# A gated cross-attention block with a routed FFN: another order of the last tiles, and other ends of the attention

## The chip, the cores and the metric

The program runs on one core of one Trainium2 chip. The metric is the device time of one execution in microseconds. An execution of the kernel before took 836.75 us in the median of three runs (835.48 to 837.84).

## The reference, cut to what matters

```python
# x, ctx: (16, 256, 256); 16 heads of 16; E = 8 experts, TOP_K = 2, H = 1024; all float32
x = x + tanh(g_xattn[0]) * xattn(layernorm(x), ctx, ctx)
x = x + tanh(g_ffn[0])   * moe(layernorm(x))

def xattn(queries, keys, values):
    q, k, v = queries @ Wq + bq, keys @ Wk + bk, values @ Wv + bv      # split in 16 heads
    attn = softmax(q @ k.T / 4)                                        # 256 x 256 for each head
    return (attn @ v) @ Wo + bo

def moe(x):                                                            # 4096 tokens
    logits = x @ Wr + br
    gate = softmax(logits where among the top 2, else -inf)
    y[e] = relu(x @ W1[e] + b1[e]) @ W2[e] + b2[e]
    return sum over e of gate[e] * y[e]
```

## The kernel before, in words

Every product that needs float32 accuracy is made of float16 matmuls of a high part and a low part: a high part is ScalarE's copy to float16, the low part VectorE's difference. "Split" below means this pair of steps.

**Attention stage.** There are 16 batches (NB) of 256 tokens. The function `body(t, par)` of each engine is one turn m = 2t+par; it works on several batches at once. In body m, maxima of the scores of batch m are taken (`scores_max` on TensorE, `reduce` on VectorE, eight steps), the attention of batch m-1 is done (`scores`, ScalarE's `exp`, `attend`, eight steps u), and for batch m-2 the result is turned back, divided, multiplied with Wo, added to x, normed, and its router logits follow (`turn_out`, `attended`, `attended_T`, `output`, `residual`, `norm2`, `norm2_T`, `router`). Maxima use PSUM banks 0-1, scores banks 2-3, `attend` bank 7. Since a step u of `scores` writes the same two banks as the step before, it waits for that step's exp. Body NB (m = 16) has no maxima; it holds the attention of batch 15, and the expert weights that arrive late are split beside it. Batch 15's own remainder follows it, written out by hand together with the first products of tile 0.

GpSimd (POOL) computes norms, adds residuals, and issues indirect DMAs: `send_entry` scatters a token and its gate to the list of its expert, `gather` fetches the normed rows of a tile by its list, `scatter` adds a tile's rows to the output in DRAM. SyncE (SP) issues the other loads and stores in a fixed order. Each engine works through its own queue in order; semaphores tie them.

**Expert stage.** The lists of the experts are cut in 32 big tiles (BIGS) of 256 rows and 7 small tiles (SMALLS) of 128. Before, tiles 0 to 31 are big and 32 to 38 small. `step(j)` of each engine does in TensorE `first(j+1)` (x by W1, eight chunks c, 6 matmuls each) interleaved chunk by chunk with `second(j-1)` (hidden by W2, 8 chunks for each 128 rows), and at chunk 4 `gathered_T(j+2)`, the transposes of a gathered tile. ScalarE applies `relu` to tile j+1 in four parts and makes the high part of tile j+2 (`high_x`). VectorE makes low parts of tile j+2 (`low_x`) and of the hidden of tile j+1 in two halves (`cut_hidden`), and computes the weighted output rows of tile j-1 from PSUM (`result`, once for each 128 rows s). `cut_hidden(j+1)` waits for the second product of tile j-1, whose buffer it overwrites. The hidden buffer halves are freed by the cuts, so `relu` waits for the cuts of the tile before.

The wait that the change touches most is in `second`: before its first chunk it waits for `y_ready`, the end of the result that last used its bank. For big tiles banks 6 and 7 hold s = 0 and 1; small tiles use 6 and 7 in turn (`y_bank`). In a step behind a small tile, `result` stands between the two halves of `cut_hidden`. POOL's step j issues `gather(j+2)`, then `scatter(j-2, 1)`, list entries in the early steps, and `scatter(j-1, 0)`, which waits until the scatter of the tile before has landed. Small tiles have buffer halves and semaphores of their own for gathers (`gather_small`, `xg_half`). At the start of each step an engine reads the expert's number of a tile from the table (`value_load`, lines 1862 and 1864 on TensorE) and addresses the weights by it. The first steps, and those from tile 30 on, are written out; the steps between are a loop.

At the start of the program the keys' product of batch 0 comes first on TensorE, then the transposes of the normed x, the queries' product, batch 1's transposes, and a small product of bv and Wo; VectorE then splits Wo before the first reduction.

Of the kernel before, what the change touches and what calls it, by code (L numbers as in the profile page):

```python
# [23 lines left out]
ALU = mybir.AluOpType  # L24
# [8 lines left out]
P = 128  # L33
# [11 lines left out]
def flamingo(nc, x, ctx_in, g_xattn, g_ffn, Wq, bq, Wk, bk, Wv, bv, Wo, bo, Wr, br, W1, b1, W2, b2, out):  # L45
# [26 lines left out]
    with ctx:  # L72
# [241 lines left out]
        xg_half = [[sem(f"xg_half{i}{h}") for h in range(2)] for i in range(2)]  # L314
# [50 lines left out]

        def lists_at(m, par, first):


            return par == first % 2 and within(m, first, NB + 1)
# [7 lines left out]
        def tiles(eng, step, extra, chain=None, per_step=0):  # L377


            laps = BIGS // 2 - 1  # L380
# [15 lines left out]

        def subs(j):

            return SUB if not isinstance(j, int) or j < BIGS else 1

        def slot_at(j):

            return SUB * j if not isinstance(j, int) or j <= BIGS else SUB * BIGS + j - BIGS

        def subs_to(lap):

            return SUB * lap if not isinstance(lap, int) or lap <= BIGS // 2 else SUB * BIGS // 2 + lap - BIGS // 2

        def half_of(j):

            return (j - BIGS) // 2 % 2

        def y_bank(j, par, s):

            return 6 + (s if subs(j) == SUB else par)
# [27 lines left out]
        def _(sp):  # L443
# [81 lines left out]
            def slot_load(j):  # L525
                wait(sp, slots_full[j % 2], 16 * (j // 2))
                base = sp.value_load(tile_base[0:1, j:j + 1], min_val=0, max_val=LISTED - subs(j) * P)
# [68 lines left out]
            for j in range(EARLY, BIGS):  # L596
                slot_load(j)
            hold(sp, table_ready, 6)
            for j in range(BIGS, NT):
                slot_load(j)  # L600

            hold(sp, y_sent[0], 16 * subs_to((NT + 1) // 2))
            hold(sp, y_sent[1], 16 * subs_to(NT // 2))


        @block.gpsimd
        def _(pool):
# [88 lines left out]
            def gather(j, lap, par):  # L696
                hold(pool, slots_full[par], 16 * (lap + 1))
                wait(pool, xg_full[par], 16 * subs_to(lap))
# [7 lines left out]

            def gather_small(j, par):
                h, turn = half_of(j), (j - BIGS) // 4
                if turn == 0:
                    hold(pool, xg_full[par], 16 * SUB * (BIGS // 2))  # L710
                    hold(pool, gT_done, BIGS - 1 + par)
                else:
                    hold(pool, xg_half[par][h], 16 * turn)
                    hold(pool, gT_done, j - 3)
                hold(pool, slots_full[par], 16 * (j // 2 + 1))
                nc.gpsimd.tensor_copy(gather_idx[par][:, h:h + 1].unsqueeze(2), slots[:, slot_at(j):slot_at(j) + 1, 0:1]).then_inc(idx_ready, 1)
                hold(pool, idx_ready, j + 1)
# [1212 lines left out]
```

## Time and profile before

| | us |
|---|---|
| median of 3 runs (lowest, highest) | 836.75 (835.48, 837.84) |
| the profiled execution | 833.6 |
| its span, first to last instruction | 831.8 |
| TensorE busy in it, over its span | 726.9 (87%) |
| VectorE busy | 609.4 (73%) |
| ScalarE busy | 406.4 (49%) |
| GpSimd busy | 458.8 (55%) |
| mean granted TensorE clock | 0.963 of full |

The profile is of one execution. Busy time of an engine is the union of its instructions; PE is TensorE's matmuls, PEld its weight loads, DVE VectorE, ACT ScalarE, POOL GpSimd. In a timeline each row begins with its start and its duration in us, then the engine, the line of kernel.py, the operation, out<-in and the count of merged instructions; brackets hold the idle time of the engine before it and what ended it. A q behind an engine's name is its sequencer. PEclk is the TensorE clock that was granted, 1.00 being 2.4 GHz and 0.50 1.2 GHz.

### The profile page before, as it was taken

How to read it: one execution, taken by the hardware profiler on the slowest of the kernel's cores; microseconds unless marked ns; L12 is line 12 of the kernel's file. 1: busy time of each engine (PE TensorE's matmuls, PEld its weight loads, DVE VectorE, ACT ScalarE, POOL GpSimd, SP SyncE). 2: the span in 40 equal slices, each digit the busy share in tenths (PEclk: the TensorE clock that was granted, in tenths of full speed). 3: DMA queues.
4: the chain of work that ended last, by engine and by line, in shares of the span. 5: the costliest groups of instructions: out<-in, count | busy, mean ns of one | idle time of the engine just before them, and what ended most of it. 6: DMA issues, size and time to landing. Idle time of an engine off the chain costs nothing.

```text
span 831.8 us, 21356 instructions
## 1 busy us (share of the span) xinstructions
PE 726.9 (87%) x6536; PEld 488.2 (59%) x6537; DVE 609.4 (73%) x1256; ACT 406.4 (49%) x783; POOL 458.8 (55%) x453
## 2 busy tenths in 40 slices
PE   2679999888888888877879999999999999999982
PEld 2335555454555544433657777777777777777761
DVE  5668888889898889996356787667666666676653
ACT  2256777677776767675333333333333333333330
POOL 6224444566565676437447677755655555556522
PEclk9689999999999999997689999999999999999997
DMA  6436656676767665553312232343232222333321
GB/s 188 121 85 207 187 162 183 164 191 173 187 154 172 185 183 162 155 141 114 69 49 46 40 52 46 52 54 52 46 48 46 44 48 46 50 50 49 44 32 20
DMA packets 96790, 85.32 MB, mean 103 GB/s; under 512 B 22257, under 2 KB 86001, under 8 KB 96593
## 3 DMA queue, kind: packets, MB, share of 16 engines
q1 hardware_dynamic: 80752, 65.73, 29.1%
q0 software_dynamic: 15680, 18.69, 14.2%
q8 instruction: 41, 0.67, 0.3%
q14 instruction: 29, 0.23, 0.1%
q10 hardware_dynamic: 288, 0.00, 0.0%
HBM read 53.61 MB, written 30.62 MB: 101 GB/s over the span
## 4 chain that ended last, share of the span: by engine, by line
PE 41%; DVE 19%; issue 16%; DMA 9%; POOL 8%; ACT 4%; POOLq 1%; DVEq 0%; ACTq 0%; SPq 0%
PE banks L1765 10%; DMA out_dram<-yb,dest_idx 7%; DVE negmax L1119 7%; PE banks L1661 5%; POOL xg L704 4%; PE banks L1747 4%; PE banks L1749 4%; PE banks L1748 4%; PE banks L1577 3%; ACT probs L931 2%; PE banks L1649 2%; PE banks L1563 2%; POOL out_dram L778 2%; DVE stats L1043 2%; PE banks L1702 2%
## 5 line engine op out<-in xcount | busy, mean ns | idle before, releaser
L994 ACT ACTIVATE hid<-banks,b_col 128x256 f32<-128x256 f32 (+1 forms) x312 | 124.2, 452 | 219.3 <-PE banks L1749 112.9
L1765 PE MATMUL banks<-wall,hh 128*128 x568 | 204.8, 380 | 1.4 <-DVE hl L1458 1.0
L778 POOL DMA_INDIRECT out_dram<-yb,dest_idx x71 | 124.8, 1757 | 126.8 <-DMA out_dram<-yb,dest_idx 58.5
L1119 DVE TENSOR_REDUCE negmax<-banks 128x4 f32<-128x1024 f32 x128 | 155.7, 1217 | 20.7 <-PE banks L1628 20.0
L1747 PE MATMUL banks<-xh,wall 128*128 128x256 f16 (+1 forms) x624 | 163.2, 266 | 5.2 <-ACT hid L994 4.3
L931 ACT ACTIVATE probs<-banks 128x1024 f32<-128x1024 f32 x128 | 131.1, 1024 | 71.8 <-PE banks L1649 70.8
L1749 PE MATMUL banks<-xh,wall 128*128 128x256 f16 (+1 forms) x624 | 163.2, 266 | 0.0
L1748 PE MATMUL banks<-xl,wall 128*128 128x256 f16 (+1 forms) x624 | 163.2, 266 | 0.0
L1765 PE MATMUL banks<-wall,hl 128*128 x568 | 144.3, 273 | 0.0
L1661 PE MATMUL banks<-probs,vaug 128*32 128x256 f32 x1024 | 84.4, 402 | 26.1 <-ACT probs L931 15.3
L689 POOL DMA_INDIRECT token_lists<-entry,place_i x64 | 69.2, 1082 | 66.4 <-ACT probs L931 41.9
L704 POOL DMA_INDIRECT xg<-xn_rows,gather_idx x64 | 77.8, 1215 | 30.4 <-issue 18.1
L1458 DVE TENSOR_TENSOR hl<-hid,hh 128x1024 f16<-128x1024 f32 (+1 forms) x78 | 88.2, 1130 | 2.7
L1507 DVE SCALAR_TENSOR_TENSOR yb<-banks,b_b 128x256 f32<-128x256 f32 x71 | 30.1, 424 | 74.1 <-PE banks L1765 73.8
L1748 PEld LDWEIGHTS banks<-xl,wall 128*128 x624 | 61.6, 99 | 33.0 <-issue 0.3
L1765 PEld LDWEIGHTS banks<-wall,hh 128*128 128x128 f16 x568 | 55.6, 98 | 30.9 <-issue 2.5
L1747 PEld LDWEIGHTS banks<-xh,wall 128*128 x624 | 61.8, 99 | 14.7 <-issue 7.2
L1628 PE MATMUL banks<-ks,qs 48*128 48x256 f16 x512 | 51.0, 278 | 22.1 <-DVE negmax L1119 21.8
L628 POOL TENSOR_TENSOR var_eps<-mean_var,eps_col 128x2 f32<-128x2 f32 x32 | 7.1, 223 | 106.9 <-DVE mean_var L1048 106.9
L1749 PEld LDWEIGHTS banks<-xh,wall 128*128 x624 | 61.7, 99 | 6.6
L1765 PEld LDWEIGHTS banks<-wall,hl 128*128 128x128 f16 x568 | 55.7, 98 | 13.0 <-issue 0.3
L1456 DVE CAST hh<-hid 128x1024 f16<-128x1024 f32 (+1 forms) x78 | 50.8, 651 | 9.2 <-PE banks L1765 7.8
(203 smaller groups left out, 1177.6 us busy)
## 6 DMA issues: line engine op xcount, KB each, us to landing
raw<-in_L_ffn_W SPq DMA_DIRECT2D x16, 512.0 KB, 5.7
wst<-in_L_ffn_W SPq DMA_DIRECT2D x16, 512.0 KB, 6.4
k_parts<-kparts SPq DMA_DIRECT2D x48, 128.0 KB, 5.5
q_parts<-qparts SPq DMA_DIRECT2D x48, 128.0 KB
ks<-k_parts SPq DMA_DIRECT2D x64, 96.0 KB, 2.3
qs<-q_parts SPq DMA_DIRECT2D x64, 96.0 KB, 2.2
xin<-in_x SPq DMA_DIRECT2D x16, 256.0 KB, 2.9
cin<-in_ctx SPq DMA_DIRECT2D x16, 256.0 KB, 3.3
```

Source lines behind the costliest of these rows:

```text
L689: nc.gpsimd.indirect_dma_start(list_d, bass.IndirectOffsetOnAxis(place_i[:, kk, i:i + 1], 0), entry[:, kk, i, :], None).then_inc(list_sent ...
L704: nc.gpsimd.indirect_dma_start(xg[par][:, s, :], None, rows, bass.IndirectOffsetOnAxis(gather_idx[par][:, s:s + 1], 0)).then_inc(xg_full[p ...
L778: nc.gpsimd.indirect_dma_start(out_rows, bass.IndirectOffsetOnAxis(dest_idx[par][:, s:s + 1], 0), yb[par][:, s, :], None, compute_op=ALU.a ...
L931: nc.scalar.activation(probs[v % 2][:].rearrange("p h t -> p (h t)"), banks[:, 2:4, :].rearrange("p b t -> p (b t)"), ACT.Exp, scale=float ...
L994: ins = nc.scalar.activation(hid[half][:, c % (HC // 2), 0:subs(j) * P], banks[:, b, c % 2 * TS:c % 2 * TS + subs(j) * P], ACT.Relu, bias= ...
L1119: nc.vector.tensor_reduce(negmax[:, c, 8 * (g // 2):8 * (g // 2) + 8].rearrange("p (m g p2) -> p m g p2", m=2, g=2)[:, :, g % 2, :], banks ...
L1458: nc.vector.tensor_tensor(hl[par][:, cs, 0:rows], hid[half][:, :, 0:rows], hh[par][:, cs, 0:rows], ALU.subtract).then_inc(hl_ready, 1)
L1661: ins = nc.tensor.matmul(banks[32 * j:32 * j + 32, 7, 0:L], vaug[par][:, c, 8 * (j // 2) + 2 * g + j % 2, :], probs[v_ % 2][:, j, :], star ...
L1747: nc.tensor.matmul(dst, hi, xh[par][:, m, 0:rows], start=(m == 0), stop=False)
L1748: nc.tensor.matmul(dst, hi, xl[par][:, m, 0:rows], start=False, stop=False)
L1749: ins = nc.tensor.matmul(dst, lo, xh[par][:, m, 0:rows], start=False, stop=(m == M - 1))
L1765: ins = nc.tensor.matmul(dst, h_[:, c, s * P:(s + 1) * P], w_, start=(c == 0 and k == 0), stop=(c == HC - 1 and k == 1))
```

## The change

The expert stage:

- Tiles 0 to 24 are big; from tile 25 on small and big tiles alternate (25, 27, ... 37 small, 26, 28, ... 38 big). `MIXED` is 25. The table keeps its order; `entry_of(j)` finds the entry of tile j. The loop ends at tile 22, later steps are written out.
- Results of s = 0 are always in bank 6, those of s = 1 in bank 7; `y_bank` goes. `second` waits for the result of the tile before in the same bank.
- `gather(j+3)` is issued in POOL's step j, behind `scatter(j-2, 1)` and the list entries, ahead of `scatter(j-1, 0)`. `gather_small` and its semaphores go.
- In a step behind a small tile, VectorE's `result` stands behind both halves of `cut_hidden`.
- `gathered_T` stands at chunk 2 instead of 4 where tile j+1 is small.

The end of the attention:

- In body NB the scores alternate between banks 2-3 and 0-1, and `scores(u+1)` is issued before `attend(u)`; `gathered_T(0)` moves from step 6 to 3, ScalarE's `high_x(0)` from 7 to 5. ScalarE's copy for the router (`norm2_T`) and `spread` leave the body. The late weight splits 6 and 7 are one or two steps later.
- POOL's `residual(14)` is ahead of two entry sends.
- Behind the body, the first products of tile 0 are spread between `turn_out`, `norm2_T`, `attended_T`, `router` and `output`; `low_x(1)` comes ahead of the statistics of batch 15; `high_x(1)` ahead of the last `relu`.

The start:

- Norm transposes of batch 0 are ahead of its keys' product; the bv by Wo product moves ahead of batch 1's transposes and to bank 7; statistics of batch 1 are earlier.
- The maxima of batch 0 alternate between banks 0-1 and 2-3, each waiting for the reduction two steps back.
- Splitting Wo moves into body 0, behind its sixth reduction; `output(0)` waits for it instead of `v(0)`.

```diff
+        def score_bank(m, v):
+            return 2 if not isinstance(m, int) or m < NB or v % 2 == 0 else 0
+        def out_bank(n, c):
+            return 5 + c if not isinstance(n, int) or n < NB - 1 or c == 0 else 3
+        def max_bank(n, w):
+            return 2 if isinstance(n, int) and n == 0 and w % 2 else 0
...
-            laps = BIGS // 2 - 1
+            laps = (MIXED - 2) // 2
...
+        MIXED = NT - 2 * SMALLS
+        def smalls_to(j):
+            return max(0, j - MIXED + 1) // 2 if isinstance(j, int) else 0
         def subs(j):
-            return SUB if not isinstance(j, int) or j < BIGS else 1
+            return 1 if isinstance(j, int) and j >= MIXED and (j - MIXED) % 2 == 0 else SUB
...
+        def entry_of(j):
+            return j - smalls_to(j) if subs(j) == SUB else BIGS + smalls_to(j)
...
+                last = isinstance(m, int) and m == NB
+                if last:
+                    residual(m - 2)
                 if sending:
                     paced(here[0], 0)
                     paced(here[1], 2)
-                if post:
+                if post and not last:
                     residual(m - 2)
...
-                if not fixed or 2 <= j < BIGS - 2:
-                    gather(j + 2, t + 1, i)
-                elif j >= BIGS - 2:
...
+                if there(j, 3) and not (fixed and j < 1):
+                    gather(j + 3, t + 1 + i, 1 - i)
                 if there(j, -1):
                     scatter(j - 1, 1 - i, 0, t + (i - 1) // 2)
...
             relu(0, e, 0)
+            relu(0, e, 1)
+            norm2_T(NB - 2)
             attended_T(NB - 1)
-            for b in range(1, 4):
-                relu(0, e, b)
+            relu(0, e, 2)
             high_x(1, 1)
+            relu(0, e, 3)
+            spread(NB // 2 - 2)
...
             dve.wait_ge(biases_ready, 1)
+            norm1_stats(1, 0, 1)
+            norm_low(0)
             k_low(0, 5)
-            norm_low(0)
-            norm1_stats(1, 0, 1)
             q_low(0, 6)
             context_low(1, 1)
+            norm_low(1)
             split_whole(wv, xres, wv_full, wv_high, wv_split)
-            norm_low(1)
...
+                    if w == 5 and isinstance(m, int) and m == 0:
+                        output_weights()
...
             attended(n, 1)
-            router(n - 1, 0, 7)
             attended_low(n)
             cut_hidden(0, 0, 0)
+            router(n - 1, 0, 7)
             residual(n)
+            low_x(1, 1)
             norm2_stats(n)
             cut_hidden(0, 0, 1)
-            low_x(1, 1)
...
                 for half in range(2):
                     if there(j, 1):
                         cut_hidden(j + 1, 1 - i, half)
-                    if half == 0 and after_small and there(j, -1):
-                        result(j - 1, (j - 1) // 2, 1 - i, 0, e)
+                if there(j, -1) and after_small:
+                    result(j - 1, t + (i - 1) // 2, 1 - i, 0, e)
...
-                wait(pe, mx_red, 8 * n + w)
+                wait(pe, mx_red, 8 * n + w if not isinstance(n, int) or n else w - 1)
...
+                if v_ == 0 and isinstance(n, int) and n == 0:
+                    pe.wait_ge(mx_red, 8)
+                if not isinstance(n, int) or n < NB - 1 or v_ == 0:
+                    wait(pe, exp_done, 8 * n + v_)
+                elif v_ == 1:
+                    pe.wait_ge(mx_red, 8 * NB)
+                else:
+                    pe.wait_ge(exp_done, 8 * n + v_ - 1)
...
-                    if subs(j) == SUB:
-                        wait(pe, y_ready, slot_at(j - 1) + s + 1)
-                    else:
-                        pe.wait_ge(y_ready, slot_at(j - 2) + 1 if j - 2 >= BIGS else slot_at(BIGS - 1) + 1 + par)
+                    wait(pe, y_ready, slot_at(j - 1) + (s + 1 if s < subs(j - 1 if isinstance(j, int) else j) else 0))
...
+            norm_T(0)
             for m in range(M):
                 k(0, 0, m, 5)
-            norm_T(0)
...
+                last = isinstance(m, int) and m == NB
                 for u in range(8):
-                    if attention:
+                    if last and u == 0:
+                        scores(m - 1, 1 - par, 0)
+                    if last and u < 7:
+                        scores(m - 1, 1 - par, u + 1)
+                    elif attention and not last:
                         scores(m - 1, 1 - par, u)
...
-            turn_out(n, 0)
-            turn_out(n, 1)
-            router(n - 1, None, 7)
             pe.wait_ge(table_ready, 2)
             pe.wait_ge(late_lo, len(LATE))
             e = pe.value_load(tile_expert[0:1, 0:1], min_val=0, max_val=E - 1)
             first(0, 0, e, 0)
             first(0, 0, e, 1)
-            attended_T(n)
+            turn_out(n, 0)
+            turn_out(n, 1)
             first(0, 0, e, 2)
             first(0, 0, e, 3)
+            norm2_T(n - 1)
+            attended_T(n)
+            first(0, 0, e, 4)
+            first(0, 0, e, 5)
+            router(n - 1, None, 7)
             output(n, 0)
             output(n, 1)
-            for c in range(4, HC):
-                first(0, 0, e, c)
             gathered_T(1, 0, 1)
+            first(0, 0, e, 6)
+            first(0, 0, e, 7)
...
-                    if there(j, 2) and c == HC // 2:
+                    if there(j, 2) and c == (HC // 2 if not isinstance(j, int) or subs(j + 1) == SUB else 2):
```

## Rows read from the trace of the kernel before

**Rows 1.** the page: engines' busy time (share), and the last chain by engine

```profile
PE 726.9 (87%) x6536; PEld 488.2 (59%) x6537; DVE 609.4 (73%) x1256; ACT 406.4 (49%) x783; POOL 458.8 (55%) x453
...
PE 41%; DVE 19%; issue 16%; DMA 9%; POOL 8%; ACT 4%; POOLq 1%; DVEq 0%; ACTq 0%; SPq 0%
```

**Rows 2.** stages: busy us (count) of PE, PEld, DVE, ACT, POOL; PEclk, DMA share, GB/s

```profile
377.40:402.60 25.20, 18.39 (x139) 8.87 (x138) 11.98 (x31) 14.72 (x22) 19.04 (x23) 0.70 0.31 83
402.60:429.90 27.30, 21.71 (x154) 18.30 (x155) 13.17 (x26) 8.83 (x21) 9.40 (x14) 0.81 0.29 78
429.90:761.70 331.80, 329.67 (x2539) 248.99 (x2540) 227.04 (x472) 116.94 (x271) 204.70 (x166) 1.00 0.30 47
...
778.00:811.50 33.50, 29.24 (x327) 21.92 (x324) 19.61 (x48) 13.53 (x45) 12.07 (x10) 1.00 0.26 34
```

**Rows 3.** timeline, TensorE, big tiles: start us, us, what, [idle before <-releaser]

```profile
691.26 0.60 PE L1733 MATMUL banks<-ident,xg 128*128 128x128 f32 x4
...
702.13 0.60 PE L1733 MATMUL banks<-ident,xg 128*128 128x128 f32 x4
```

**Rows 4.** timeline, TensorE, two small steps

```profile
781.10 0.38 PE L1733 MATMUL banks<-ident,xg 128*128 128x128 f32 x2
...
788.06 0.38 PE L1733 MATMUL banks<-ident,xg 128*128 128x128 f32 x2
```

**Rows 5.** a table load (line L1864) and the weight loader, in one small step's boundary

```profile
L1864 PEldq TENSOR_LOAD <-tile_expert x1: 296/296/296, 783.6 to 783.6; - x1
...
784.40 0.10 PEld L1747 LDWEIGHTS banks<-xh,wall 128*128 x1 [1.33 <-issue]
```

**Rows 6.** timeline, VectorE and ScalarE, around the last big tile but one

```profile
751.09 0.42 DVE L1507 SCALAR_TENSOR_TENSOR yb<-banks,b_b 128x256 f32<-128x256 f32 x1 [2.59 <-PE banks L1765]
...
752.41 0.69 DVE L1456 CAST hh<-hid 128x1024 f16<-128x1024 f32 x1
...
754.27 0.69 DVE L1456 CAST hh<-hid 128x1024 f16<-128x1024 f32 x1
...
754.49 0.84 ACT L994 ACTIVATE hid<-banks,b_col 128x256 f32<-128x256 f32 x2 [3.11 <-DVE hl L1458]
```

**Rows 7.** timeline, VectorE, one small tile

```profile
783.57 0.43 DVE L1456 CAST hh<-hid 128x512 f16<-128x512 f32 x1 [1.21 <-PE banks L1765]
...
784.64 0.21 DVE L1505 TENSOR_SCALAR dest_f<-slots,filler 128x1 f32<-128x1 f32 x1
...
786.19 0.42 DVE L1456 CAST hh<-hid 128x512 f16<-128x512 f32 x1
```

**Rows 8.** what the gathered transposes (L1733) waited for in the tile stage: us, times

```profile
  DMA xg<-xn_rows,gather_idx: 5.7, 9
```

**Rows 9.** stretches of 4 us between attention and tiles, columns as in rows 2

```profile
414.00:418.00 4.00, 1.47 (x14) 1.15 (x11) 3.23 (x8) 2.02 (x5) 2.27 (x3) 1.00 0.82 295
418.00:422.00 4.00, 3.35 (x21) 2.48 (x22) 0.59 (x1) 0.36 (x1) 3.51 (x4) 0.63 0.18 63
...
426.00:430.00 4.00, 2.00 (x17) 1.66 (x15) 3.90 (x7) 1.42 (x4) 0.00 (x0) 0.91 0.00 0
430.00:434.00 4.00, 4.00 (x22) 2.57 (x22) 3.18 (x20) 0.43 (x2) 1.89 (x2) 0.66 0.02 4
```

**Rows 10.** timeline, last batch: an exp on ScalarE, and TensorE before the first ranks

```profile
389.77 1.02 ACT L931 ACTIVATE probs<-banks 128x1024 f32<-128x1024 f32 x1 [1.06 <-PE banks L1649]
...
418.65 0.19 PE L1710 MATMUL banks<-picked,tri 128*128 128x32 bf16 x1 [3.18 <-DVE xl L1447]
```

**Rows 11.** timeline, the end: VectorE after step 37, the last scatter on POOL

```profile
811.50 0.43 DVE L1456 CAST hh<-hid 128x512 f16<-128x512 f32 x1 [3.02 <-PE banks L1765]
...
823.51 1.54 POOL L778 DMA_INDIRECT out_dram<-yb,dest_idx  x1 [3.05 <-DMA out_dram<-yb,dest_idx]
```

**Rows 12.** timeline, TensorE, maxima of batch 0 and of batch 1

```profile
26.21 0.39 PE L1628 MATMUL banks<-ks,qs 48*128 48x256 f16 x4 [1.53 <-DVE negmax L1119]
...
41.93 0.61 PE L1628 MATMUL banks<-ks,qs 48*128 48x256 f16 x4 [0.99 <-DVE negmax L1119]
```

More of the change, by code:

```diff
@@ L595, in _ @@
             hold(sp, table_ready, 4)
-            for j in range(EARLY, BIGS):
+            for j in range(EARLY, MIXED):
                 slot_load(j)
             hold(sp, table_ready, 6)
-            for j in range(BIGS, NT):
+            for j in range(MIXED, NT):
                 slot_load(j)
-            hold(sp, y_sent[0], 16 * subs_to((NT + 1) // 2))
-            hold(sp, y_sent[1], 16 * subs_to(NT // 2))
+            hold(sp, y_sent[0], 16 * subs_to((NT + 1) // 2, 0))
+            hold(sp, y_sent[1], 16 * subs_to(NT // 2, 1))
         @block.gpsimd
@@ L968, in body @@
                             values(m, par)
+                        if isinstance(m, int) and m == NB:
+                            high_x(0, 0)
                     elif v == 6:
@@ L973, in body @@
                     elif v == 7:
-                        if isinstance(m, int) and m == NB:
-                            high_x(0, 0)
-                        if post:
+                        if post and not (isinstance(m, int) and m == NB):
                             norm2_T(m - 2)
@@ L981, in body @@
                     copy_out(3)
-                if lists_at(m, par, LEAD):
+                if lists_at(m, par, LEAD) and within(m, 0, NB - 1):
                     spread(t - 2)
@@ L1088, in attended @@
                 dve.wait_ge(tok_done, 2 * n + c + 1)
-                rows = bank(5 + c).rearrange("p (h w) -> p h w", w=32)
+                rows = bank(out_bank(n, c)).rearrange("p (h w) -> p h w", w=32)
                 link(nc.vector.reciprocal(recip[c][:].unsqueeze(2), rows[:, :, DH:DH + 1]))
@@ L1500, in result @@
                 if s == 0:
-                    wait(dve, y_sent[par], 16 * subs_to(lap))
+                    wait(dve, y_sent[par], 16 * subs_to(lap, par))
                     dve.wait_ge(slots_full[par], 16 * (lap + 1))
@@ L1682, in output @@
                     pe.wait_ge(cT_split, n + 1)
+                    if isinstance(n, int) and n == 0:
+                        pe.wait_ge(wo_split, 1)
                 i = 0
@@ L1816, in body @@
                             output(m - 2, 0)
+                        if last:
+                            gathered_T(0, 0, 0)
                     elif u == 4:
@@ L1829, in body @@
                         attend(m - 1, 1 - par, u)
-                    if u == 6 and isinstance(m, int) and m == NB:
-                        gathered_T(0, 0, 0)
-                    if u == 7 and post:
+                    if u == 7 and post and not last:
                         norm2_T(m - 2)
```

108 lines of the change are left out of this document (40 added, 68 removed).

## The prediction

> **What bounds the kernel now.** I read the page first: TensorE is busy 87% of the span, and the chain that ended last runs 41% over it [rows 1]. Then the stages [rows 2]: in the expert stage up to 761.7 it is busy 329.67 of 331.80 us, so there only TensorE work counts. The time that can move lies at its two ends. In the last seven tiles (all small) it is busy 29.24 of 33.50 us; in the last attention batch 18.39 of 25.20 us at a granted clock of 0.70; between attention and the steady tiles 21.71 of 27.30 at 0.81.
>
> Two big tiles in a step (first product of tile j+1, second of tile j-1) take 10.87 us between one set of transposes and the next [rows 3]. Without some 0.44 us of transposes (0.60 with the pipeline's latency) that is 1.30 us for each of eight chunks, half of it (0.65) from either product. In a small step both halve: 0.66 x 8 + 0.22 = 5.5 us. The trace shows 6.96 [rows 4], 1.46 more. The weight loader stands 1.33 us at the boundary, with nothing the profile names as releaser, while the sequencer runs two table loads, of which one is shown [rows 5]. In a big step the queued matmuls cover them. That pause stands four times behind small steps, 5.8 us in all.
>
> **The new tile order.** Small tiles are now 25, 27, ... 37. Since a step joins j+1 and j-1, steps do not mix sizes: even steps 26 to 36 are small with small, odd ones big with big. TensorE work is unchanged. What changes is a wait: all results of s=0 now use bank 6, so `second` of a big tile behind a small one waits at its first chunk for the small tile's result, and the change puts that result last on VectorE, behind both cuts. Before, small tiles took banks 6 and 7 in turn and this wait fell a step later.
>
> I follow one pair from t=0, the end of a big step. VectorE first finishes that step's second result, 1.3 us (751.09 to 752.41), and cuts the big tile, 1.86 a half [rows 6]: 5.1. ScalarE's activations of the small tile wait for those halves, as at 754.49 [rows 6], so the next split of x ends near 5.9. TensorE's small step ends at 5.7 and only that releases the small cuts. These take 1.07 each (783.57 to 784.64), the result 1.55 (784.64 to 786.19) [rows 7]: 5.9 + 2.1 + 1.6 + wake-ups 0.3 = 9.9. TensorE wants to start that product at 5.7 + 0.65 = 6.35. It stands 3.6 us, which includes the table-load pause. Queued behind the waiting matmul are all other first products of the step, so nothing fills the hole. Six pairs: +21.6. Gone are the four old pauses: -5.8. Bounds for a pair: 1.5 (only the old pause) and 4.2 (slower ScalarE links).
>
> **The end.** The last tile is now big: 2.6 us of its second product move behind step 37, so that step ends 2.6 earlier. Before, step 37 ended at about 811.4 (VectorE starts at 811.50), the last scatter was issued at 823.51, and the span ended 8.3 later [rows 11]: 20.4. Now, from the end of step 37: result 1.4, two big cuts 3.7, small result 1.6, wake 0.2 = 6.9; second product 5.3 = 12.2; last half result 1.4 and wake 0.2 = 13.8; last scatter, then 8.3: 22.1. So +1.7 - 2.6 = -0.9. A scatter waits for the landing of the tile before (1.54 + 3.05 us [rows 11]); that stays inside this chain. Bounds -2.6 and +1.5.
>
> **Gathers three ahead.** `gather(j+3)` stands behind `scatter(j-2, 1)` instead of `gather(j+2)` before it, and is a step earlier. The copy of indices, two gathers of about 1.1 us each and the entry sends share the POOL queue, busy 204.70 of 331.80 us in the tile stage [rows 2]; slot loads on SP come one tile earlier and were far ahead. The loader waited for gathers nine times, 5.7 us in all [rows 8]; the matmuls already queued cover about half. I take -2.9; bounds 0 and -5.7.
>
> **The clock.** After a stretch of 4 us with 1.47 us busy, TensorE's granted clock fell from 2.4 to 1.2 GHz (0.63 in the next stretch), and again after 2.00 of 4 busy (0.66) [rows 9]. A new hole is 3.6 us idle with one chunk inside it, of the same kind. The mean of 0.63 over 4 us is about 3 us at half clock; work done in it takes 1.5 to 1.7 longer. Behind it the big step is TensorE-bound, so the loss stays: 6 x 1.7 = +10.2. Bounds 0 and +16.
>
> The Trainium skill ("TensorE: Matmul & The Clock Gate", section "HAM oscillation") describes a kernel that goes back to the slow clock in every tile because of a wait between bursts. That rule speaks against this change; without it the sum would be 10.2 lower, with it as above. The trace agrees as far as the two stretches show.
>
> **The last attention batch.** In batch 15's attention the maxima are done, so scores alternate between banks 2-3 and 0-1 and are issued a turn ahead. Before, each exp waited for its scores: 1.06 us idle before an exp of 1.02 [rows 10], about 2.1 a turn, 2.4 with a copy-out. Now exps follow at ScalarE's pace, 1.0 to 1.4 a turn. Five late turns save about 4; the gathered transposes move from turn 6 to 3 and no longer stand before the last scores (1.5); the last copy-out is not behind the router's activation copy (0.8); 0.7 more in the early turns: -7. TensorE still has router and transposes in turns 0 to 2, and the product with Wo in turn 3 waits for VectorE's late weight split, so it is not more. POOL's residual moves ahead of two entry sends; those were not waited for.
>
> Behind it, first products of tile 0 are put between `turn_out`, `attended_T`, `router` and `output`, each of which waited for ScalarE or VectorE, and the split of tile 1 comes before the statistics and the last cut. At 418.65 TensorE had waited 3.18 us for that split [rows 10]. This wait goes almost wholly; some 2 us of half clock go with the denser work: -5. Late next is the norm of batch 15: VectorE's statistics, then POOL's norm, then router 15 before step 1, so of step 0 only 1 us goes. Together -13. Bounds -5 (clock low all through) and -16.
>
> **The start.** Maxima of batch 0 alternate between two bank pairs, which removes waits as that of 1.53 us before the second [rows 12]; VectorE becomes the bound, with eight reductions, its splits, and now the five operations of the output weights between the sixth and the seventh instead of ahead of the first. Batch 0's scores come earlier by about 1.4, and the 0.99 us wait of batch 1's first maxima [rows 12] goes: -2.4. Norm before keys shortens the query chain, but the first matmuls at half clock come later too; I count nothing for it. Bounds +1 and -5.
>
> **The sum**, against the profiled execution (span 831.8, 833.6 with what lies around it): 21.6 - 5.8 - 0.9 - 2.9 + 10.2 - 13 - 2.4 = +6.8, so 840.4. The median shown is 3.15 above that execution; on it, 836.75 + 6.8 = 843.5.
>
> **Rivals.**
> A. The clock stays up through the holes. For it: the old pauses of 1.3 us left it at 1.00 [rows 2]. Against: rows 9. It decides at whether the hole counts as one. 843.5 - 10.2 = 833.3, just faster than before.
> B. The result of a small tile doesn't hold TensorE, because VectorE gets to it in time. For it: VectorE is busy only 20 of 33.5 us in the small stage [rows 2]. Against: the order of its queue. It decides if the result is out by 6.4 us of the pair. Then holes and clock loss go: 843.5 - 21.6 - 10.2 = 811.7; with old pauses in six small steps 818.
> C. The two ends give little, since each is held by a chain that moves only as a whole (row loads on SP at the start, POOL's norm at the end): -5 in place of -15.4. 854.
> D. The edits at the attention's ends change nothing at all, and clock loss is at its upper bound: 865. I give it almost nothing.
>
> **Chances.** Forecast 0.50, own range 838 to 849. A 0.20 (829 to 837). B 0.12 (808 to 822). C and D 0.18 (849 to 862). The range 829 to 855 leaves out B, and half of C: 0.2. From no change 0.3% (2.5 us, about what can be told here) gives the limits 834.2 and 839.3. Faster: B, a bit over half of A, a little of the forecast: 0.26. Same: 0.14. Slower: 0.60.
>
> **What would show it.** In the changed kernel's trace: six waits of `second` on VectorE's result behind small tiles, each 2 to 3 us after a table pause of about 1, with pair periods near 20 us or 21.7 with the clock; granted clock below 1.00 in stretches from step 27 on; no waits on gathers; exps of the last batch following at 1.0 to 1.4 us; the first ranks of the tile stage 12 to 15 us earlier relative to the start. It is wrong if the pair period stays below 18.5 us, or if the ends give under 8 us or over 20.

## The result and the profile after

The changed kernel takes 851.95 us (median of 4 runs, 849.88 to 853.39), the kernel before 837.07 on the same chip (4 runs, 835.48 to 837.84): ratio 1.0178, 95% interval 1.0150 to 1.0206, 14.9 us slower. I had forecast +6.8. The direction was right, the size was not. The profiled execution takes 852.82 us, its span is 850.7 and its mean granted clock 0.954.

The page of the changed kernel: TensorE's row, the last chain by engine (to be read against [rows 1]), and the group of second-product matmuls.

```profile
PE 735.8 (86%) x6536; PEld 488.5 (57%) x6537; DVE 604.0 (71%) x1256; ACT 404.6 (48%) x783; POOL 461.4 (54%) x453
...
PE 57%; DVE 26%; issue 9%; ACT 3%; DMA 1%; POOL 1%; DVEq 1%; SPq 0%; POOLq 0%; ACTq 0%
...
L1769 PE MATMUL banks<-wall,hh 128*128 x568 | 211.8, 392 | 22.7 <-DVE yb L1515 22.7
```

The same 6536 matmuls are busy 8.9 us longer, and the second product now waits 22.7 us for VectorE's `yb`, the result, which the group of before didn't. Both belong to the tile order. Next, the timeline of TensorE: five of the six waits that I had counted behind small tiles, then the seventh, behind the last small tile and ahead of the last tile.

```profile
703.92 0.57 PE L1769 MATMUL banks<-wall,hh 128*128 x1 [3.20 <-DVE yb L1515]
...
725.63 0.60 PE L1769 MATMUL banks<-wall,hh 128*128 x1 [3.01 <-DVE yb L1515]
...
748.43 0.61 PE L1769 MATMUL banks<-wall,hh 128*128 x1 [3.09 <-DVE yb L1515]
...
792.84 0.60 PE L1769 MATMUL banks<-wall,hh 128*128 x1 [3.10 <-DVE yb L1515]
...
814.48 0.61 PE L1769 MATMUL banks<-wall,hh 128*128 x1 [3.00 <-DVE yb L1515]
...
834.05 0.61 PE L1769 MATMUL banks<-wall,hh 128*128 x1 [4.30 <-DVE yb L1515]
```

From 703.92 to 792.84 lie four pairs, 22.2 us each (forecast 20, or 21.7 with the clock). The product itself lasts 0.6, where it lasts 0.39 at full clock (e3 and e9 below). VectorE ahead of the wait at 748.43:

```profile
743.60 0.68 DVE L1451 SCALAR_TENSOR_TENSOR xl<-banks,xh 128x512 f16<-128x512 f32 x1
744.39 0.43 DVE L1460 CAST hh<-hid 128x512 f16<-128x512 f32 x1
744.85 0.69 DVE L1462 TENSOR_TENSOR hl<-hid,hh 128x512 f16<-128x512 f32 x1
745.46 0.42 DVE L1460 CAST hh<-hid 128x512 f16<-128x512 f32 x1
745.91 0.69 DVE L1462 TENSOR_TENSOR hl<-hid,hh 128x512 f16<-128x512 f32 x1
746.52 0.21 DVE L1509 TENSOR_SCALAR dest_f<-slots,filler 128x1 f32<-128x1 f32 x1
...
747.81 0.35 DVE L1515 TENSOR_SCALAR yb<-yb,slots 128x256 f32<-128x256 f32 x1
```

Two cuts, then the result, with no idle time between: the chain of my forecast. The stages after, with the columns of [rows 2]: up to tile 25's transposes, up to the first wait, the six pairs, the end.

```profile
421.20:670.70 249.50, 248.27 (x1917) 188.16 (x1918) 172.34 (x379) 87.34 (x203) 160.24 (x135) 0.99 0.33 48
670.70:703.90 33.20, 29.81 (x273) 22.61 (x271) 22.59 (x46) 11.54 (x32) 17.95 (x15) 1.00 0.31 49
703.90:834.00 130.10, 109.26 (x840) 77.19 (x840) 63.46 (x132) 35.87 (x98) 49.99 (x41) 0.88 0.22 33
834.00:850.70 16.70, 6.86 (x32) 3.55 (x32) 2.76 (x8) 0.00 (x0) 4.66 (x3) 0.70 0.21 25
```

A mean of 0.88 over 130.1 us, at levels of 1.0 and 0.5, is 31 us at half clock, 5.2 a pair. It comes in pieces of two lengths in turn, as behind the first and the second wait:

```profile
703.00:708.00 5.00, 4.08 (x19) 2.48 (x20) 0.53 (x2) 0.84 (x2) 3.58 (x4) 0.66 0.31 45
724.00:732.00 8.00, 6.37 (x28) 3.80 (x29) 1.30 (x4) 0.84 (x2) 3.76 (x4) 0.57 0.27 51
```

That is 3.4 us at half clock behind one wait and 6.9 behind the next. The kernel before, from its tile 25's transposes to its end, for the same 1144 or 1145 matmuls:

```profile
680.30:831.80 151.50, 132.00 (x1144) 98.36 (x1144) 91.11 (x187) 49.20 (x130) 73.65 (x60) 0.97 0.28 42
```

After, the same stretch (the last three stages above) takes 180.00 us, with TensorE busy 145.93. So of 28.5 us more, in 13.9 TensorE is busy longer with the same matmuls, and 14.6 are idle time.

From the profile after alone the ends seem to give little: tile 1's first product starts at 421.20, 8.7 us earlier than before (429.90 in [rows 2]; I had forecast 15.4), and there is a new wait in the last attention batch. First that wait, then exps of batch 15 on ScalarE after, then the first and the last of them before:

```profile
390.03 1.25 PE L1698 MATMUL banks<-wo,cT 128*128 128x256 f16 x5 [3.53 <-DVE cT L1069]
```

```profile
380.40 1.02 ACT L929 ACTIVATE probs<-banks 128x1024 f32<-128x1024 f32 x1
...
387.98 1.02 ACT L929 ACTIVATE probs<-banks 128x1024 f32<-128x1024 f32 x1
...
393.75 1.02 ACT L929 ACTIVATE probs<-banks 128x1024 f32<-128x1024 f32 x1
...
396.59 1.03 ACT L929 ACTIVATE probs<-banks 128x1024 f32<-128x1024 f32 x1
```

```profile
379.19 1.03 ACT L931 ACTIVATE probs<-banks 128x1024 f32<-128x1024 f32 x1
...
398.46 1.02 ACT L931 ACTIVATE probs<-banks 128x1024 f32<-128x1024 f32 x1 [2.86 <-PE banks L1649]
```

Five exps follow the one before at 1.2 to 1.9 us, one after 2.71 and one only after 5.77: 16.2 us from first to last, where it was 19.3. One trace is a weak measure of the ends, though: the profiled execution of before was 3.5 us faster than its median.

### The profile page after: what moved, and what is told of

The parts are those of the page before. It is cut to its first block, busy times and chain, and to the rows that moved or that the text cites. A ratio compares the mean times of both kernels' runs of the same rounds, so it can differ in the third digit from the quotient of the medians.

```text
span 850.7 us, 21021 instructions
## 1 busy us (share of the span) xinstructions
PE 735.8 (86%) x6536; PEld 488.5 (57%) x6537; DVE 604.0 (71%) x1256; ACT 404.6 (48%) x783; POOL 461.4 (54%) x453
## 4 chain that ended last, share of the span: by engine, by line
PE 57%; DVE 26%; issue 9%; ACT 3%; DMA 1%; POOL 1%; DVEq 1%; SPq 0%; POOLq 0%; ACTq 0%
PE banks L1769 20%; PE banks L1757 7%; PE banks L1755 6%; DVE negmax L1120 6%; PE banks L1756 6%; PE banks L1671 4%; PE banks L1581 3%; DVE hl L1462 2%; PE banks L1659 2%; DVE hh L1460 2%; ACT probs L929 2%; PE banks L1567 2%; PE banks L1714 2%; DVE stats L1044 2%; PE banks L1631 2%
## 5 line engine op out<-in xcount | busy, mean ns | idle before, releaser
L1769 PE MATMUL banks<-wall,hh 128*128 x568 | 211.8, 392 | 22.7 <-DVE yb L1515 22.7
L1120 DVE TENSOR_REDUCE negmax<-banks 128x4 f32<-128x1024 f32 x128 | 155.5, 1217 | 22.6 <-PE banks L1631 22.2
L1769 PE MATMUL banks<-wall,hl 128*128 x568 | 148.8, 281 | 0.0
L1671 PE MATMUL banks<-probs,vaug 128*32 128x256 f32 x1024 | 84.0, 400 | 23.0 <-ACT probs L929 14.6
L718 POOL DMA_INDIRECT xg<-xn_rows,gather_idx x71 | 82.2, 1158 | 26.7 <-issue 15.5
L1659 PE MATMUL banks<-qs,ks 49*128 49x256 f16 x512 | 51.1, 280 | 1.9 <-DVE negmax L1120 1.9
```

The lines of the kernel that those rows point to most:

```text
L718: nc.gpsimd.indirect_dma_start(xg[par][:, s, :], None, rows, bass.IndirectOffsetOnAxis(gather_idx[par][:, s:s + 1], 0)).then_inc(xg_full[p ...
L1120: nc.vector.tensor_reduce(negmax[:, c, 8 * (g // 2):8 * (g // 2) + 8].rearrange("p (m g p2) -> p m g p2", m=2, g=2)[:, :, g % 2, :], banks ...
L1671: ins = nc.tensor.matmul(banks[32 * j:32 * j + 32, 7, 0:L], vaug[par][:, c, 8 * (j // 2) + 2 * g + j % 2, :], probs[v_ % 2][:, j, :], star ...
L1769: ins = nc.tensor.matmul(dst, h_[:, c, s * P:(s + 1) * P], w_, start=(c == 0 and k == 0), stop=(c == HC - 1 and k == 1))
```

## The experiments

Unless said otherwise, a number is the ratio to the kernel before with its 95% interval (5 rounds). 0.001 is 0.84 us. Each kernel ran beside the kernel before, on several chips in all; where I give a difference of two kernels, it is that of their ratios.

**Which part costs what.** Two kernels split the change in two: `e1_ends` takes the start and the last attention batch from the changed kernel and leaves tile order and gathers as before; `e2_tiles` does the reverse.

> The kernel before with the changed start and the changed last attention batch with what follows it, and with its own tile order and gathers (two ahead, seven small tiles last). The trace of the changed kernel has its first second-product matmul of tile 0 8.7 us earlier than the trace of the kernel before, where I had forecast 15.4. Theory: these two parts give 8.7 wherever the tile stage stands, so 837.1 - 8.7 = 828.4. Rival: the gathers three ahead or the tile order took part of it away again, then 837.1 - 15.4 = 821.7. Second rival: what the start gives is lost inside the attention stage for good, and only the last batch counts: -6, 831.

> The kernel before with only the new tile order and the gathers three ahead. By the traces the stage from tile 25's transposes to the end is 28.5 us longer in the changed kernel and the stage before it 0.9 shorter: 837.1 + 27.6 = 864.7. My forecast had +22.2 for these parts (holes 21.6, pauses -5.8, end -0.9, gathers -2.9, clock 10.2): 859.3. If the medians count and not the two traces, 851.95 + 8.7 = 860.7.

e1_ends: 0.9829 (0.9801 to 0.9858), -14.3 us. e2_tiles: 1.0336 (1.0302 to 1.0370), +28.1 us. The sum, +13.8, agrees with +14.9. So the ends gave nearly what I had forecast (-15.4), more than the profile after alone let expect; the tile stage costs 28 in place of 22.2.

Two more kernels take the start alone and the attention's end alone.

> The kernel before with only the changed start (order of the first projections, maxima of batch 0 in two bank pairs, output weights split later). My forecast: -2.4, bounds +1 and -5: 0.9971 of before. By the traces batch 1's first exp comes 2.8 us earlier in e1_ends and 2.0 in the changed kernel: -2.4. Rival: what the start gives is taken back inside the attention stage, as in the changed kernel's trace, where 2.0 us at batch 1 are 0.5 at batch 12: -0.5, 0.9994.

> The kernel before with only the changed last attention batch and what follows it. My forecast: -13, bounds -5 and -16: 0.984 of before. From e1_ends (-14.2 for both parts) less 2.4 for the start: -11.8, 0.986. Rival: the gain of the last batch is smaller than that and the start's larger, since the half-clock stretches at the start move: -9, 0.989.

e7_start_only: 0.9975 (0.9964 to 0.9987), -2.1 us (forecast -2.4). e8_attention_end_only: 0.9892 (0.9869 to 0.9916), -9.0 us (forecast -13). Together these are -11.1, 3.2 short of e1's -14.3, which is about what the three intervals allow; by e1 less e7 the attention's end gives -12.2.

**The waits in the pairs.** In `e3_result_first` the small result stands ahead of the cuts, in `e9_result_between` between them. The edit of e3:

```
-                for half in range(2):
-                    if there(j, 1):
-                        cut_hidden(j + 1, 1 - i, half)
                 if there(j, -1) and after_small:
                     result(j - 1, t + (i - 1) // 2, 1 - i, 0, e)
+                for half in range(2):
+                    if there(j, 1):
+                        cut_hidden(j + 1, 1 - i, half)
```

> The changed kernel with the small tile's result put ahead of both cuts on VectorE. Theory: the six holes of 3.3 to 3.5 us are VectorE's two small cuts before the result. Then a hole shrinks to result and wake-up less 0.65, about 1.3 us or the table-load pause of 1.3: -2.0 x 6 = -12, and if the granted clock then stays at 1.00 through the pairs, 2.5 a pair more, -15: 852.0 - 27 = 825. Rival (the clock falls with the short holes too): 840. Rival (the holes wait for something else than the order, as the x split or the table loads): no change, 852.

> The changed kernel with the small tile's result between the two cuts of the small tile on VectorE (in the changed kernel it stands behind both, in e3_result_first ahead of both). One cut of 1.07 us less stands ahead of it, so the holes should be 3.35 - 1.1 = 2.2 to 2.3 us: -6.6 in six pairs. It tells at what length the granted clock falls: with holes of 1.3 us it stayed, with 3.3 it fell each time. If it falls at 2.3 too: 852.0 - 6.6 = 845 (1.010 of before). If it stays: -12.5 more, as e5_hole_filled measured, 833 (0.995).

e3_result_first: 0.9846 (0.9814 to 0.9878), 27.8 us faster than the changed kernel by one edit. e9_result_between: 1.0034 (1.0009 to 1.0060), 12 faster. One wait of each kernel, e3 then e9, each followed by a stretch of pairs of that kernel (columns of [rows 2]; in e3 exactly five pairs, 17.95 us each):

```profile
730.72 0.39 PE L1769 MATMUL banks<-wall,hh 128*128 x1 [0.98 <-DVE yb L1515]
```

```profile
694.80:784.60 89.80, 83.64 (x751) 63.11 (x752) 56.53 (x116) 32.51 (x90) 46.65 (x39) 1.00 0.28 44
```

```profile
741.03 0.39 PE L1769 MATMUL banks<-wall,hh 128*128 x1 [2.13 <-DVE yb L1515]
```

```profile
701.00:822.00 121.00, 105.00 (x842) 75.61 (x843) 64.55 (x135) 35.96 (x98) 50.54 (x42) 0.92 0.24 36
```

Each cut ahead of the result adds about its 1.07 us to the wait: 0.98, 2.13, 3.1. The clock stays at 1.00 with waits of 1.0, is 0.92 with waits of 1.9 to 2.1 and 0.88 with 3.0 to 3.2. Neither of my two expectations for e9 was met: 1.0034 lies between 0.995 and 1.010, since half-clock stretches still came, but less of them (0.92 over 121 us is 19 us at half clock, against 31). The length of a wait alone doesn't decide: behind e9's first wait, of 2.03 us, the clock stayed at 1.00 up to the next, and so did the product behind e2's first wait, of 3.10 us, last 0.39.

`e4_result_other_bank` keeps VectorE's order and lets small tiles use bank 7, so the big tile behind waits only at its second half. The edit of the waits, condensed:

```
+        def y_bank(j, s):
+            return 6 + (s if subs(j) == SUB else 1)
-                    wait(pe, y_ready, slot_at(j - 1) + (s + 1 if s < subs(j - 1 ...) else 0))
+                    if subs(j) == 1: pe.wait_ge(y_ready, slot_at(j))
+                    elif isinstance(j, int) and subs(j - 1) == 1: pe.wait_ge(y_ready, slot_at(j - 1) + s)
+                    else: wait(pe, y_ready, slot_at(j - 1) + s + 1)
```

> The changed kernel with the small tile's result in bank 7 (the big tile's second half uses it), in VectorE's order as changed. The big tile behind it then waits for the small result only at its second half, about 5 us later. Theory (the shared bank is the wait): holes shrink to the table-load pause, 1.3 us, clock stays up: 852.0 - 12 - 15 = 825. But the small tile's own second product now waits for the second half of the big tile before it, which VectorE reads out about 1.3 us into the step: a wait of up to 0.7 us in six small steps, 829. Rival (the clock loss is of another origin): 840.

0.9858 (0.9821 to 0.9894), as the theory has it. The waits of 3.1 are gone from its trace. In each pair the small tile's own product now waits 1.24 us for the big tile's result (I had allowed 0.7), and 0.7 is left at the boundary behind the small step; the granted clock is 0.99 over 690 to 820. Order and shared bank are two ways to take away the same wait.

**The clock by itself.** `e5_hole_filled` keeps the wait and gives TensorE something to do in it. Its edit, with the line that picks the weights `idle` left out:

```
+                    if s == 0 and isinstance(j, int) and subs(j) == SUB and subs(j - 1) == 1:
+                        pe.wait_ge(y_ready, slot_at(j - 1))
...
+                        for _ in range(12):
+                            nc.tensor.matmul(banks[:, 7, 0:2 * D], hh[par][:, 0, 0:P], idle, start=True, stop=True)
                     wait(pe, y_ready, ...)
```

> The changed kernel, with 12 extra matmuls of 512 columns (0.22 us each at full clock, 2.6 us) into bank 7 ahead of each wait of a big tile's second product on a small tile's result; they compute nothing that is used. The wait itself and its length stay: the next product starts when VectorE's result is there, as before. It prices the granted clock alone. Theory: the clock falls because TensorE stands idle in the hole, and at 14.7 us (six intervals of 3.4 or 6.8 us at half clock, 30.7 us in all, half of it lost) it is larger than the 10.2 that I had put in: 1.018 x before falls to 852.0 - 14.7 = 837, as before. If my price of 1.7 a hole was right: 842. Rival: the clock falls for another reason than the idle time, or does not cost time: 852.

1.0029 (1.0011 to 1.0046): 12.5 us faster than the changed kernel, with 84 matmuls added (12 ahead of each of seven big tiles). The stretch with the pairs:

```profile
700.00:820.00 120.00, 114.29 (x936) 79.90 (x934) 67.42 (x141) 37.68 (x104) 51.64 (x42) 1.00 0.25 38
```

Granted clock 1.00, and the pairs are 19.8 us each from one such product to the next, against 22.1. In the six pairs the added matmuls end 0.2 to 0.4 us before the product starts, so they don't hold it up. Ahead of the last tile they do:

```profile
819.58 4.45 PE L1769 MATMUL banks<-wall,hh 128*128 x12 [2.64 <-DVE hl L1462]
```

There they run mostly at half clock and the product follows at 823.87, where VectorE had the result out at 820.98. So 12.5 us is rather too low for what the clock costs. The intervals of the two ratios leave it uncertain by some 3 us; my 10.2 is within that, but the traces speak for more (below).

**The gathers.** `e6_ends_gathers3` is e1_ends with `gather(j + 3)` behind the second scatter; `e10_gathers_two_ahead` is the changed kernel with `gather(j + 2)` at the head of POOL's step.

> The kernel of e1_ends (new start and new last attention batch, old tile order) with the gathers of big tiles issued three tiles ahead, behind the second scatter, as in the changed kernel. It prices that edit. My forecast: -2.9, bounds 0 and -5.7, so 0.3% under e1_ends, 817.4 beside 820.3. By the traces (tile 0's first second-product to tile 25's transposes: 249.2 before, 248.3 and 247.9 with three ahead, 249.3 in e1_ends) it is -1.1: 819.2. Rival: it costs, since a scatter now stands behind two gathers on POOL's queue: over 820.5.

> The changed kernel with the gathers two tiles ahead, at the head of POOL's step, as before the change. Forecast by my step: without the three-ahead edit +2.9, 855. By e6_ends_gathers3 (no difference from e1_ends): 852, 1.018 of before. By the stage up to tile 25, which is 1.0 us shorter in the two traces with three ahead: 853. Rival: with tiles of two sizes in turn, two ahead is too late for the small steps and TensorE waits for gathers: over 856.

e6: 0.9834 (0.9808 to 0.9859), no difference from e1_ends that the intervals show (some 3 us either way). What the transposes waited for between tile 0's second product and the last tiles: two rows of e1_ends; e6 has no row on `xg` there except POOL's own.

```profile
PEld banks L1762 <- DMA xg<-xn_rows,gather_idx: 4.3, 9, 0.8
...
PE banks L1762 <- DMA xg<-xn_rows,gather_idx: 0.4, 1, 0.4
```

The loader's 4.3 us of waits went and the time didn't move: queued matmuls covered all but the 0.4 in which TensorE itself is named. e10: 1.0249 (1.0197 to 1.0300), 6 slower than the changed kernel, the interval wide (5 us either way). Its trace shows why: in the new order two ahead is late for the small steps, and TensorE waits six times for a gather, 7.2 us in all. So the new order needs the gathers three ahead, which the old one doesn't.

```profile
693.34 0.66 PE L1741 MATMUL banks<-ident,xg 128*128 128x128 f32 x4 [0.87 <-DMA xg<-xn_rows,gather_idx]
...
701.53 0.60 PE L1769 MATMUL banks<-wall,hh 128*128 x1 [2.51 <-DVE yb L1515]
...
718.46 0.66 PE L1741 MATMUL banks<-ident,xg 128*128 128x128 f32 x4 [2.11 <-DMA xg<-xn_rows,gather_idx]
```

**The table-load pause.** In two kernels TensorE's queue keeps the number it loaded for tile j+1 and uses it two steps later as that of tile j-1 (the edit of e12, condensed).

```
                 if there(j, -1):
-                    e2 = pe.value_load(tile_expert[0:1, ds(j - 1, 1)], ...)
+                    e2 = kept[j - 1] if isinstance(j, int) and j - 1 in kept else pe.value_load(...)
+                if isinstance(j, int) and j >= BIGS - 2: kept[j + 1] = e1 if there(j, 1) else None
```

> The kernel of e1_ends (new start, new last attention batch, old tile order), with the kept register from step 30 on. It has five pauses of 1.31 to 1.41 us in its small steps. Theory (table loads): -3 to -5, 816 (0.978). Rival (the pause has another origin): 820.3, 0.983.

> The kernel of e3_result_first, and in the unrolled steps from 22 on TensorE's queue keeps the expert number of tile j+1 in its register for step j+2, so one table load a step is left in place of two. Theory: the pause of 1.2 to 1.4 us at each of the six small-to-big boundaries is the two table loads that the queued matmuls of a small step do not cover; with one load it is half or nothing: -4 to -7, 816 (0.977). Rival: one load alone costs as much as two, or the pause is the wait for VectorE's result, 1.3 by my reckoning: 822 (0.985).

e12 (old order): 0.9798 (0.9755 to 0.9841), 2.6 us under e1, uncertain by 4. Its small steps, from transposes to transposes:

```profile
771.85 0.38 PE L1762 MATMUL banks<-ident,xg 128*128 128x128 f32 x2
...
777.43 0.38 PE L1762 MATMUL banks<-ident,xg 128*128 128x128 f32 x2
...
783.71 0.38 PE L1762 MATMUL banks<-ident,xg 128*128 128x128 f32 x2
...
790.07 0.38 PE L1762 MATMUL banks<-ident,xg 128*128 128x128 f32 x2
```

They are 5.58, 6.28 and 6.36 us, where [rows 4] have 6.96 and e1's trace 6.95, 7.08 and 6.94; my step without pause was 5.5. With one load less the whole pause goes in the first and about half of it in the other two. e11 (new order, result first): 0.9835 (0.9796 to 0.9875), no gain over e3: its trace still has six waits of 1.0 to 1.1 at the boundary, for the result.

**The late attention batches.** In the changed kernel's trace the new wait of 3.53 goes back to one weight split on VectorE, with POOL's residual beside it, which the change moved ahead of two entry sends:

```profile
384.81 1.22 DVE L1171 SCALAR_TENSOR_TENSOR wall<-raw,wall 128x1024 f16<-128x1024 f32 x1
...
386.26 3.11 DVE L1171 SCALAR_TENSOR_TENSOR wall<-wst,wall 128x1024 f16<-128x1024 f32 x1
386.99 1.28 POOL L667 TENSOR_TENSOR xres<-xres,out_bias 128x512 f32<-128x512 f32 x1
```

`e13` undoes that move in e8, `e14` in e12, `e15` in the changed kernel, `e16` in e3.

```
-                last = isinstance(m, int) and m == NB
-                if last:
-                    residual(m - 2)
                 if sending:
                     paced(here[0], 0)
                     paced(here[1], 2)
-                if post and not last:
+                if post:
                     residual(m - 2)
```

> The kernel of e8_attention_end_only with POOL's residual of batch 14 back behind the two entry sends. In the traces of the changed kernel and of five others with that edit, one weight split on VectorE in the last attention batch takes 3.10 to 3.12 us where it takes 1.22 elsewhere, each time while POOL's residual (1.28 us) runs beside it; behind it stand the split of the attended values and TensorE's product with Wo. My forecast priced the move of the residual at 0. Theory (the two hold each other up): -1.9 from 0.9892, so 0.987, and all splits are at 1.2. Rival A: the residual now runs beside another operation of VectorE and stretches that, or makes the next norm late: 0.989. Rival B: the long split had nothing to do with POOL and stays at 3.1.

> The same edit undone in the kernel of e12_ends_and_kept_register, the fastest so far (0.9798): by the theory -1.9 and 0.9776, 816; by rival A no change, 0.980.

> The changed kernel, whole, with only POOL's residual of batch 14 back behind the two entry sends. The same edit gave -5.0 us in two other kernels (0.9892 to 0.9832 and 0.9798 to 0.9738). If it is a term of its own in the changed kernel: 1.0178 - 0.006 = 1.012, 847. Rival: the time is given back in front of the holes, since VectorE's chain there has its own pace: 1.018, 852.

> The changed kernel with both edits: the small tile's result ahead of the cuts (as e3_result_first, 0.9846) and POOL's residual back. If the two terms add: 0.9846 - 0.006 = 0.979, 817. It would show the new tile order with neither of the two costs, beside e14 (old order, 0.9738 with the kept register). Rival: they overlap, 0.984.

e13: 0.9832 (0.9810 to 0.9855), -5.0 us against e8. e14: 0.9738 (0.9716 to 0.9760), -5.0 against e12. But e15: 1.0184 (1.0161 to 1.0207), nothing, and e16: 0.9871 (0.9848 to 0.9894), 2 slower than e3, which is within the intervals. The long split is gone in all four traces. VectorE in e13:

```profile
385.00 1.22 DVE L1184 SCALAR_TENSOR_TENSOR wall<-wst,wall 128x1024 f16<-128x1024 f32 x1
386.14 0.68 DVE L1083 TENSOR_TENSOR cT<-banks,cT 128x512 f16<-128x512 f32 x1
386.74 1.69 DVE L1218 SCALAR_TENSOR_TENSOR masked<-onehot,logits 128x32 f32<-128x32 f32 x1
```

The split is at 1.22 again and the residual now stretches an operation of 128x32 to 1.69, behind which nothing urgent stands; the product with Wo waits 1.35 in e13 and 0.55 in e15. Two things keep this from being a fixed term. The long split stands in seven of the traces with the moved residual (the changed kernel, e1, e6, e8, e10, e11, e12), and in four it doesn't (e3, e4, e5, e9), though their instructions there are those of the changed kernel: whether the two operations meet like this is a matter of the execution. And the clock differs. The stretch from batch 14's first exp to tile 0's second product, in e13, in e15, in the changed kernel and in the kernel before:

```profile
354.20:416.30 62.10, 49.51 (x469) 31.69 (x469) 48.30 (x109) 38.84 (x65) 40.57 (x44) 0.93 0.46 121
```

```profile
353.50:420.20 66.70, 55.27 (x470) 34.19 (x469) 49.34 (x109) 39.10 (x65) 39.91 (x44) 0.83 0.41 112
```

```profile
353.50:422.50 69.00, 52.35 (x470) 32.32 (x469) 49.74 (x110) 39.05 (x64) 41.02 (x44) 0.89 0.39 109
```

```profile
353.90:431.10 77.20, 58.21 (x469) 36.51 (x469) 47.90 (x111) 38.89 (x65) 37.96 (x44) 0.81 0.37 99
```

Here TensorE is busy 75 to 83% of the time and its granted clock lies between 0.81 and 0.93. e3, with the instructions of the changed kernel up to the tiles, runs through this stretch in 64.1 us at 0.92. What sets the clock there I have not found, so what the residual's move costs the changed kernel stays open: between 0 and 5 us.

## Why the forecast had the sign and missed the size

In us, forecast against measured (each part by its ratio, in brackets by the trace):

```
start and last attention batch     -15.4    -14.3   e1
  start alone                       -2.4     -2.1   e7
  attention's end alone            -13       -9.0   e8 (-14.0 with the residual back, e13)
tile order and gathers             +22.2    +28.1   e2
  six waits behind small tiles     +21.6    (+18.4: 22.7 less the 4.3 of the last tile)
  clock                            +10.2    +12.5   e5 (+13.9 by the stage's busy time)
  gathers three ahead               -2.9      0     e6 on e1
  old pauses gone                   -5.8    not run alone
  end                               -0.9    not run alone
whole                               +6.8    +14.9
```

The mechanism was right. Big steps behind small ones wait for the small tile's result; the cause is its place on VectorE (e3, e9) together with the shared bank (e4), and the clock falls with the waits (e5). Without these two costs the new order ends at 0.9846 (e3), 1.4 us behind the old order with the same ends (e1). Rival B, with its 811.7 or 818, is thus nearly what one other line order gives; it was wrong of this kernel. Rival A is refuted by the 0.88. Rival C's 854 is near the measured time by luck: it had the ends at -5, and e1 shows -14.3.

What failed is two terms of the sum for the tile stage, the clock above all, both taken too favourably:

- **Gathers three ahead, -2.9.** I took half of the loader's waits on gathers [rows 8] to reach TensorE. None that can be measured did (e6, interval some 3 us either way; in the traces the stretch from tile 0's second product to tile 25's transposes is 0.9 us shorter after than before): in a stage where TensorE is busy 329.67 of 331.80 us [rows 2], at most the 2.1 us left could come back. That bound stood in my own rows and I didn't apply it.
- **The clock, +10.2.** I read [rows 9] as about 3 us at half clock for a wait and a loss of 1.7. The changed kernel shows 3.4 and 6.9 us in turn, 5.2 a pair, and TensorE is busy 13.9 us longer for the same work: 12.6 up to the last wait, 1.3 in the last tile, for which I had put no clock at all. e5 gives 12.5, uncertain by 3.

The waits were 3.1 each, not 3.6. But the idle time of the stage as a whole came out as forecast: 21.6 - 5.8 - 0.9 = 14.9, and the traces show 14.6; which of the three terms made up for the waits was not measured. Of the 8.1 us by which the whole was missed, 3.7 are thus the clock's (by the traces; 2.3 by e5), 2.0 to 2.9 the gathers', 1.1 the ends'. The rest is within the intervals of the runs and I assign it to nothing.

The attention's end was forecast at -13 and gave -9.0 alone, -12.2 beside the new start. Its exps did not follow at 1.0 to 1.4 us: the forecast had 7 less for the batch, and the traces have 3.1 less in the changed kernel (19.3 to 16.2). From the last exp to tile 0's second product it is 32.7 us before and 25.9 after, 6.8 less, where I had 6. The step "POOL's residual moves ahead of two entry sends; those were not waited for" looked at who waits for the sends, and not at what runs beside the residual on VectorE. The local cost is seen in the traces: a split of 1.22 us takes 3.11, and the product with Wo waits 3.53. That it's a term of the changed kernel's total isn't: e15 gave nothing back.

The fastest kernel of the study is e14: old tile order, new ends, residual left in its place, one table load less: 0.9738 of the kernel before, 0.957 of the changed one.

## What to carry to other kernels

When a consumer's output buffer becomes shared between neighbouring steps, walk the reader's queue: here each operation ahead of the read added its full duration to the wait, and moving the read to the front was worth 28 us, more than the change of both ends. Bound what an edit can give back by the idle time of the engine that limits the stage, before you price the waits of the engines around it. When an operation moves on one engine, look at what then runs beside it on the others, not only at who waits for it.

## What the runs showed of the hardware

- Waits of TensorE of 1.0 us, one in 17.95, leave the granted clock at 1.00 (e3); waits of 1.9 to 2.1 give 0.92 (e9) and of 3.0 to 3.2 give 0.88 over the pairs, with 3.4 and 6.9 us at half clock in turn. One wait of 2.03 (e9) and one of 3.10 (e2), each the first of its kernel, left it at full. Matmuls of no use in the waits bring it back to 1.00, and the kernel is 12.5 us faster for doing more (e5). The Trainium skill ("TensorE: Matmul & The Clock Gate", section "HAM oscillation") describes a kernel that falls back to the slow clock in every tile; all six pairs of the changed kernel did.
- A `scalar_tensor_tensor` on VectorE beside a `tensor_tensor` of 1.28 us on POOL: 3.11 us in place of 1.22 (128x1024), 1.69 for one of 128x32 whose neighbours of that shape take 0.18 to 0.19. It stands in seven of eleven traces with the moved residual.
- With one table load in place of two behind a small step, the step takes 5.58, 6.28 and 6.36 us (e12) where it takes 6.95, 7.08 and 6.94 with two (e1).
